# Attention setup of a two-layer megakernel: order of the first loads and of the small bias products

## The reference

```python
mod = (_silu(L0_c) @ L0_wmod).reshape(L0_c.shape[0], 6, 1, -1)
sa, ca, ga, sb, cb, gb = (mod[:, i] for i in range(6))
ga = (2 * (ga >= 0) - 1) * jnp.maximum(jnp.abs(ga), 0.25)
h = _layernorm(x, axis=-1) * (1 + ca) + sa
# attention, dk = 256
q = (h @ Wq + bq) / jnp.sqrt(dk); k = h @ Wk + bk; v = h @ Wv + bv
weights = softmax(causal(q @ k.T)); ctx = weights @ v
x = x + ga * (ctx @ Wo + bo)
```

## Time and profile before

| what | value |
|---|---|
| median of 3 runs | 918.71 us |
| lowest and highest run | 917.11, 919.54 us |
| profiled execution: span from first to last instruction | 911.5 us |
| TensorE busy | 831.9 us (91%) |
| VectorE busy | 652.8 us (72%) |
| ScalarE busy | 474.6 us (52%) |
| GpSimd busy | 379.5 us (42%) |
| mean granted TensorE clock | 0.958 of full speed |

### The profile page before, as it was taken

The page is one execution under the profiler, slowest core; times in us unless marked ns, Lnnn a source line. Parts: engine busy times, 40 slices in busy tenths (PEclk is TensorE's granted clock), DMA queues, the critical chain, the costliest instruction groups (busy, mean ns, idle before and its releaser), DMA issues.

```text
span 911.5 us, 16937 instructions
## 1 busy us (share of the span) xinstructions
PE 831.9 (91%) x5115; PEld 744.7 (82%) x5115; DVE 652.8 (72%) x1917; ACT 474.6 (52%) x1006; POOL 379.5 (42%) x427
## 2 busy tenths in 40 slices
PE   6899999999999978889868999999698899988997
PEld 5789998987999877778758999999577788876776
DVE  3666677735567676878784676576768999888986
ACT  2443343434334338777724676466344345449883
POOL 3542200169000014564642445475678886423230
PEclk9799999989999995999998999999899999999999
DMA  9200000000000004242335445334411200000112
GB/s 306 104 1 1 2 1 1 2 1 1 1 1 1 2 22 136 89 140 89 112 112 148 126 129 179 103 112 133 128 47 47 65 29 1 1 1 24 47 47 70
DMA packets 47799, 58.31 MB, mean 64 GB/s; under 512 B 5599, under 2 KB 42848, under 8 KB 47712
## 3 DMA queue, kind: packets, MB, share of 16 engines
q1 hardware_dynamic: 39856, 39.11, 14.5%
q0 software_dynamic: 6480, 16.92, 5.1%
q10 hardware_dynamic: 1376, 1.20, 0.4%
HBM read 34.91 MB, written 23.22 MB: 64 GB/s over the span
## 4 chain that ended last, share of the span: by engine, by line
PE 32%; DVE 15%; issue 6%; ACT 5%; POOL 2%; SPq 1%; DMA 0%; DVEq 0%; ACTq 0%; POOLq 0%
PE bank L80 7%; PE bank L82 7%; PE bank L81 7%; PE bank L1701 2%; PE bank L1709 2%; PE bank L1600 1%; DVE xm L2090 1%; PE bank L1717 1%; PE bank L1721 1%; PE bank L1718 1%; PE bank L1719 1%; PE bank L1720 1%; DVE st L2026 1%; ACT spare L1211 1%; DVE hth L1415 1%
## 5 line engine op out<-in xcount | busy, mean ns | idle before, releaser
L367 ACT CAST pth<-tp 128x512 fp32r<-128x512 f32 (+3 forms) x80 | 41.7, 525 | 128.8 <-PE tp L717 127.4
L1144 POOL DMA_INDIRECT results<-row_tiles,idu x71 | 70.0, 986 | 89.0 <-ACT row_tiles L1293 75.0
L1128 POOL DMA_INDIRECT region<-row_tiles,posu x64 | 66.3, 1035 | 59.8 <-DVE posu L1399 42.7
L547 DVE TENSOR_TENSOR ptl<-tp,pth 128x512 fp32r<-128x512 f32 (+3 forms) x80 | 48.2, 607 | 54.7 <-ACT pth L367 54.6
L80 PE MATMUL cx<-vh,pth 128*128 128x256 f32 x272 | 80.6, 296 | 1.4 <-DVE ptl L547 1.2
L82 PE MATMUL cx<-vh,ptl 128*128 128x256 f32 x272 | 76.8, 282 | 0.0
L81 PE MATMUL cx<-vl,pth 128*128 128x256 f32 x272 | 76.8, 282 | 0.0
L80 PE MATMUL sc<-hh,ph 128*128 128x512 f32 (+3 forms) x160 | 61.0, 381 | 0.3
L82 PE MATMUL sc<-hh,pl 128*128 128x512 f32 (+3 forms) x160 | 58.3, 364 | 0.0
L81 PE MATMUL sc<-hl,ph 128*128 128x512 f32 (+3 forms) x160 | 58.1, 363 | 0.0
L358 ACT ACTIVATE prob<-sc,nmx 128x512 f32<-128x512 f32 (+3 forms) x80 | 49.4, 628 | 14.0 <-DVE nmx L520 14.0
(11 more groups left out here) (430 smaller groups left out, 2787.0 us busy)
## 6 DMA issues: line engine op xcount, KB each, us to landing
row_tiles<-region SPq DMA_DIRECT2D x71, 130.0 KB, 2.3
pairs_a<-results SPq DMA_DIRECT2D x10, 512.0 KB
x<-in_x SPq DMA_DIRECT2D x8, 512.0 KB, 10.7
out<-x SPq DMA_DIRECT2D x8, 512.0 KB, 2.9
pairs_b<-results SPq DMA_DIRECT2D x6, 512.0 KB, 4.9
early<-in_wmod SPq DMA_DIRECT2D x2, 768.0 KB, 4.6
early<-in_wmod SPq DMA_DIRECT2D x1, 1536.0 KB, 8.3
spare<-in_wg SPq DMA_DIRECT2D x8, 192.0 KB, 2.7
```

Source lines behind the costliest of these rows:

```text
L367: a_.copy(pth[:, m % 2, 0:w], tp[:, m % 2, 0:w]).then_inc(s["pt_hi"], 1)
L547: vec.tensor_tensor(ptl[:, m % 2, 0:w], tp[:, m % 2, 0:w], pth[:, m % 2, 0:w], ALU.subtract).then_inc(s["pt_lo"], 1)
L1128: g_.indirect_dma_start(region, bass.IndirectOffsetOnAxis(ap=posu[:, c, t:t + 1], axis=0), hb[:, G % HB, j], None).then_inc(scattered[G % ...
L1144: g_.indirect_dma_start(results, bass.IndirectOffsetOnAxis(ap=idu[:, j % 8:j % 8 + 1], axis=0), y[:, j % YR, 0:D], None, bounds_check=KS * ...
```

## The change

Three orders change, and no instruction is added or removed. (1) Loads: WKT goes first on SP's queue ahead of `wma`, WQT first on ACT's queue ahead of `cols`, and x of group 0 moves from SP's queue to ACT's, ahead of WQ and WK. (2) TensorE's row product stands ahead of the head products. SP's later loads now wait for `head_ready`, since the head products are now the last readers of the raw weights. (3) VectorE computes `bo_gate` and `vo_lo(1)` before `h_lo` of group 1, where they stood behind `p_lo` of group 0; ScalarE's `vo_hi(1)` moves ahead of `h_hi` of group 1 accordingly.

```diff
--- before.py
+++ after.py
@@ -215,14 +215,14 @@
                 sp.dma_start(k.x[:, G * GT:(G + 1) * GT, :],
                              d["x"][G * GW:(G + 1) * GW, :].rearrange("(t p) d -> p t d", p=P)).then_inc(x_in[G], 16)
 
+            sp.dma_start(raw[:, WKT], d["wkT"].rearrange("(c p) n -> p c n", p=P)).then_inc(w_in[WKT], 16)
             sp.dma_start(wma[:], d["wmod"][0, :, 0:3 * D].rearrange("(c p) n -> p c n", p=P)).then_inc(s["wma_in"], 16)
-            load_x(0)
             for i in (WVT, WO, WV):
                 sp.dma_start(raw[:, i], d[("wqT", "wkT", "wq", "wk", "wvT", "wo", "wv")[i]].rearrange("(c p) n -> p c n", p=P)
                              ).then_inc(w_in[i], 16)
             for G in range(1, GROUPS):
                 load_x(G)
-            sp.wait_ge(s["row_ready"], 1)
+            sp.wait_ge(s["head_ready"], 1)
             sp.dma_start(wmr[:], d["wmod"][0, :, 3 * D:6 * D].rearrange("(c p) n -> p c n", p=P)).then_inc(s["wrest_in"], 16)
             sp.dma_start(wm1[:], d["wmod"][1].rearrange("(c p) n -> p c n", p=P)).then_inc(s["wrest_in"], 16)
 
@@ -297,8 +297,10 @@
         @block.scalar
         def _(act):
             a_ = nc.scalar
+            act.dma_start(raw[:, WQT], d["wqT"].rearrange("(c p) n -> p c n", p=P)).then_inc(w_in[WQT], 16)
             act.dma_start(k.cols[:], d["cols"]).then_inc(s["cols_in"], 16)
-            for i in (WQT, WKT, WQ, WK):
+            act.dma_start(k.x[:, 0:GT, :], d["x"][0:GW, :].rearrange("(t p) d -> p t d", p=P)).then_inc(x_in[0], 16)
+            for i in (WQ, WK):
                 act.dma_start(raw[:, i], d[("wqT", "wkT", "wq", "wk")[i]].rearrange("(c p) n -> p c n", p=P)).then_inc(w_in[i], 16)
             act.dma_start(k.rows[:], d["rows"].to_broadcast([P, D + E])).then_inc(s["rows_in"], 16)
             act.wait_ge(s["cols_in"], 16)
@@ -375,6 +377,7 @@
                     act.wait_ge(s["head_ready"], 1)
                     a_.copy(voh[:, :, :, D:VW], ps_head[:, KC * B:2 * KC * B].rearrange("p (c b) -> p b c", b=B).unsqueeze(3)
                             .to_broadcast([P, B, KC, 2])).then_inc(s["u_hi"], 1)
+                    vo_hi(1)
                 else:
                     h_hi(b, 0)
                     act.wait_ge(s["drow_ready"], 1)
@@ -386,8 +389,6 @@
                         z_of(g + 2)
                     for c in range(KC):
                         p_hi(b, g, c)
-                    if b == 0 and g == 0:
-                        vo_hi(1)
                     for i in range(2):
                         if g == GPB - 1 and i == 1:
                             exp_of(b, chunks(0)[0])
@@ -488,7 +489,13 @@
             vec.tensor_tensor(vol[:, :, :, D:VW], ps_head[:, KC * B:2 * KC * B].rearrange("p (c b) -> p b c", b=B).unsqueeze(3)
                               .to_broadcast([P, B, KC, 2]), voh[:, :, :, D:VW], ALU.subtract)
             vec.tensor_copy(c0[:], ps_head[:, 2 * KC * B:2 * KC * B + B]).then_inc(s["u_done"], 1)
+            v.wait_ge(s["row_ready"], 1)
+            v.wait_ge(s["rows_in"], 16)
+            first.link(vec.tensor_tensor(bo_gate[:], ps_row.rearrange("p (b n) -> p b n", b=B),
+                                         k.rows[:, 0:D].unsqueeze(1).to_broadcast([P, B, D]), ALU.add))
+            vec.tensor_tensor(bo_gate[:], bo_gate[:], k.gate[:, 0:2], ALU.mult).then_inc(s["bo_set"], 1)
             v.wait_ge(s["u_done"], 1)
+            vo_lo(1)
 
             for b in range(B):
                 chain = Counted(v, s["dve1"], b * 5 * TPB - START)
@@ -526,13 +533,6 @@
                     if b == 0 and g == 0:
                         stats(3)
                     p_lo(b, g)
-                    if b == 0 and g == 0:
-                        v.wait_ge(s["row_ready"], 1)
-                        v.wait_ge(s["rows_in"], 16)
-                        first.link(vec.tensor_tensor(bo_gate[:], ps_row.rearrange("p (b n) -> p b n", b=B),
-                                                     k.rows[:, 0:D].unsqueeze(1).to_broadcast([P, B, D]), ALU.add))
-                        vec.tensor_tensor(bo_gate[:], bo_gate[:], k.gate[:, 0:2], ALU.mult).then_inc(s["bo_set"], 1)
-                        vo_lo(1)
                     for i in range(2):
                         if g == GPB - 1 and i == 1:
                             for m in chunks(0):
@@ -647,6 +647,10 @@
             pe.wait_ge(k.consts, 1)
             zt(0, 0)
             pe.wait_ge(s["bias_done"], 1)
+            for b in range(B):
+                for e in range(KC):
+                    last = mm(ps_row[:, b * D:(b + 1) * D], every(b123[:, 2, e, b:b + 1]), raw[:, WO, e], start=(e == 0), stop=(e == KC - 1))
+            last.then_inc(s["row_ready"], 1)
             for i, (w, of) in enumerate(((WKT, 0), (WQT, 1))):
                 for c in range(KC):
                     for e in range(KC):
@@ -657,10 +661,6 @@
                     o = 2 * KC * B + b
                     last = mm(ps_head[:, o:o + 1], every(b123[:, 0, e, b:b + 1]), b123[:, 1, e, b:b + 1], start=(e == 0), stop=(e == KC - 1))
             last.then_inc(s["head_ready"], 1)
-            for b in range(B):
-                for e in range(KC):
-                    last = mm(ps_row[:, b * D:(b + 1) * D], every(b123[:, 2, e, b:b + 1]), raw[:, WO, e], start=(e == 0), stop=(e == KC - 1))
-            last.then_inc(s["row_ready"], 1)
 
             for b in range(B):
                 def scores(m):
```

## The result

The changed kernel takes 909.29 us (median of 4 runs, 906.17 to 911.24) against 919.12 (917.11 to 922.13). The ratio, estimated from the runs of both kernels, is 0.9882, 95% interval 0.9841 to 0.9923 (the two medians alone give 0.9893). Forecast were 911.1 and 7.6 us of gain; measured are 9.8, so the time lies at the lower end of the forecast's own range of 909.3 to 913.3. The profiled execution's span is 904.4 us, 7.1 less than before's.

A forecast was written before the change was run, and what follows sets the result against it. It took TensorE, busy at full clock from 100 us, as the bound, gains coming from its earlier setup. Terms 2.2 + 3.96 + 1.4 = 7.6 us, so 918.7 - 7.6 = 911.1 us; own range 909.3 to 913.3, wider range 907.3 to 915.0.

The forecast's parts named there:

- The base: The median lies 7.2 us above the profiled span of 911.5, untouched by the change: 918.7 us.
- Part 1, start: Loads: WKT lands at about 5.0 us, so TensorE's first product starts some 4.0 us earlier.
- the unchanged x of group 1: This load lands at 14.6 us as before, half a us to either side, and `stats(1)` on VectorE waits for it.
- the term of 2.2: From the new load order, TensorE's block of small products starts at 19.4 us, 2.2 us earlier; ends 1.2 and 4.0.
- Part 2, "costs and gains nothing": Row product ahead of head products in TensorE's block of 8.52 us: same matmuls, no cost or gain by itself.
- the rival of the warm block: With the row product first, the clock holds in TensorE's block: another 2.8 us, gain 10.4, time 908.3; chance 0.09.
- The first rival: After new TensorE idling, the low clock takes in `p_of(0)`: 6.0 instead of 3.0 us, time 914.1; chance 0.13.
- the fall at 23 us: TensorE's clock at 0.52 after some 3 us of 2-column matmuls and transposes, read as following how busy it was.
- Part 3: `bo_gate` and `vo_lo(1)` fit VectorE's idle time before `h_lo`, so TensorE's 3.96 us wait before the first `v_of` goes.
- The clock term: Without the idle wait the first `v_of` takes 2.86 instead of 4.28 us: 1.4 us gained; ends -1.5 and +2.9.
- Given back later: TensorE is 96 to 99.6% busy from 100 us to the attention stage's end, so no later give-back was expected.
- The sum 7.6: Total gain from earlier loads, removed wait and clock: 2.2 + 3.96 + 1.4 = 7.6 us.

The follow-up runs named there:

- before_again: The kernel before, unedited, run again for a second trace; ratio 1.0004 (0.9968 to 1.0040) to the kernel before.
- after_again: The changed kernel, unedited, run again for a second trace; ratio 0.9880 (0.9837 to 0.9924) to the kernel before.
- gate_first: The changed kernel with VectorE's four gate operations ahead of `stats(1)` rather than behind it; ratio 0.9820 (0.9775 to 0.9865) to the kernel before.
- early pair: First traces of the kernel before and the changed kernel, both with an early clock rise; stage ends 338.44 and 328.30 us.
- late pair: Second traces of the kernel before and the changed kernel, both with a late clock rise; stage ends 346.81 and 332.93 us.
- after_third: The changed kernel, unedited, run for a third trace; median 907.92 us, ratio 0.9864 (0.9816 to 0.9911) to the kernel before.

## Why the prediction was right, point by point

- **The base.** Wrong. I took 7.2 us to lie around the span. In every profile whose own time is known it is 1.7 to 1.9 (923.4 and 925.09 for before_again). The trace of before was an unusually fast execution, by this reckoning shorter than any timed run: 911.5 + 1.7 = 913.2 against 914.13 for the fastest of 27. It had an early rise. So the terms of the sum were read from a lucky execution and taken off the median of ordinary ones.
- **Part 1, start.** The start of the first product (5.0 forecast, 4.92 measured; 4.59 to 4.97 in the other traces with these loads and no work ahead of it), the unchanged x of group 1 (14.6; 14.23 and 14.52) and VectorE's wait for it are right, and the term of 2.2 came out at 2.94, since x landed 0.4 earlier and the gate operations were 0.2 shorter. But this is the early case only. The prediction let VectorE's wait cover some 2 us of low clock in TensorE's first products; a late rise costs more than that (block at 22.22 for 18.66). Then TensorE holds the block, and the whole of the earlier landing counts: 25.82 - 22.22 = 3.6 us.
- **Part 2, "costs and gains nothing".** Wrong in the traces, and the times are too coarse to tell. The block is 2.2 us shorter, mostly because the row product runs at full clock (1.99 us for 3.76). That was most of the rival of the warm block, at 0.09, whose 908.3 is closer to the measured 909.3 than the forecast's 911.1. The first rival, a cold stretch in `p_of(0)`, came too, and smaller than its 3.0: 0.4 us here, 0.9 in after_again, 1.4 in gate_first. Net the term is 1.8 us in the early pair (11.54 for 9.72 us of block and `p_of(0)`) and 1.5 with part 2 undone.
- **What the clock follows.** The prediction took the fall at 23 us as a sign that the clock goes by how busy the engine has been. The rows say less: TensorE is shown as busy for all of that microsecond, and its timeline has no idle time since 17.89, with matmuls of 2 columns and transposes in it. Only the fall at 38 us stands behind idle time.
- **Part 3.** Right. The wait of 3.96 us is gone, nothing else took its place; undoing it brings 3.1 back in the trace and some 6 us in the times.
- **The clock term.** Sized at 1.4, as it came out in the early pair (4.28 to 2.86); in the late pair it is 5.30 - 2.86 = 2.4, and with part 3 undone it was nearly nothing (2.94). It is a draw too.
- **Given back later.** Not foreseen. I held that nothing behind the stage could absorb the gain. Nothing within the attention stage did by waiting; but the clock's falls in the later stages shift, and took 3.0, 3.5 and 1.2 us in the three traces of the changed kernel, reckoned against the first trace of before. before_again lost 3.5 in the same way without any change. Why they fall where they do is open. Nor is the clock full from 100 us to the end of the attention stage, as the prediction read from the two stretches of the earlier trace rows; between them every trace has a low stretch of some 7 us or more, here in before:

```profile
180.00:220.00 40.00, 39.44 (x233) 35.37 (x233) 19.85 (x45) 14.34 (x22) 31.25 (x32) 0.91 0.00 0
```

In the early pair the terms measure 2.94 + 1.8 + 3.96 + 1.42 = 10.1 us at the stage's end, of which 3.0 are lost behind it. The sum 7.6 was thus close to the 7.1 of that pair by two omissions that partly cancel, and that is luck; the wait of 3.96 us, its cause and the earlier start are not. The timed 9.8 us lie between this pair's 7.1 and the 13.9 by which the spans of the late pair differ (923.4 and 909.5). That most executions rise late, as eight of twelve traces did, would explain it; it is not shown, since the timed runs don't tell how they rose.

## What to carry to other kernels

Before moving an operation ask which engine is idle before it and who waits behind it: 2 us of VectorE's work, moved into a 4 us hole, were worth most of this change, since the wait cost its 4 us and then, in three of the four traces that kept it unfilled, the clock's fall behind it. Take a second trace of the kernel before, before working out a sum: one trace is one draw of the clock, and two traces of the kernel before differ by 8.4 us at the stage's end. An order of loads is worth what the next late transfer or engine allows, so look for the one that was not waited for until now.

## What the runs showed of the hardware

With the same program, the changed kernel, TensorE's first rise to full clock came once within the second group of products (L626, by 10 us) and once within the fourth (L637, after 15.2 us); the 8 matmuls of L631 between them took 1.97 us in the first case and 3.76 in the second. With 12 matmuls of the identity ahead of the first product it had come before that product in both traces. Until the first rise that it records, the clock column reads 1.00 although the matmuls run at half speed, as in the earlier trace rows at 9 to 12.5 us and here in after_third, where L631 runs:

```profile
11.50:14.90 3.40, 3.40 (x9) 2.77 (x9) 0.78 (x8) 0.00 (x0) 2.67 (x5) 1.00 1.01 331
```

There only the durations tell. The Trainium skill ("TensorE: Matmul & The Clock Gate", What's actually happening) says that the place of the rise varies by 500 ns either way; here the two executions are 5 us or more apart.
